# Attention's output phase: seven meetings of all engines a group become three, and two counters hand the work on

## The reference

```python
x = L0_attn_x                                    # 4 groups of 512 tokens, 256 channels
mod = (_silu(L0_c) @ L0_wmod).reshape(L0_c.shape[0], 6, 1, -1)
sa, ca, ga, sb, cb, gb = (mod[:, 0], mod[:, 1], mod[:, 2], mod[:, 3], mod[:, 4], mod[:, 5])
ga = (2 * (ga >= 0) - 1) * jnp.maximum(jnp.abs(ga), 0.25)
h = _layernorm(x, axis=-1) * (1 + ca) + sa
x = x + ga * _L0_attn_ref(h, ...)                # q,k,v with LoRA, RoPE, causal softmax, P.V,
                                                 # then the output projection Wo + LoRA
```

## Time and profile before

| what | value |
|---|---|
| median of 3 runs | 2363.53 us (2359.64 to 2376.82) |
| the profiled execution's own time | 2381.58 us |
| its span | 2379.8 us |
| mean granted TensorE clock | 0.907 |
| busy share of the span: PE, PEld, DVE, ACT, POOL | 83%, 68%, 71%, 61%, 40% |
| chain that ended last, by engine | PE 54%, DVE 18%, ACT 13% |
| attention's output phases, from the span's start | 178.0 to 196.4, 314.3 to 333.6, 451.0 to 469.3, 587.2 to 606.6 us |

### The profile page before, as it was taken

One profiled execution on the slowest core, in us unless ns is written; L12 is line 12 of the kernel. 1 busy time (PEld: TensorE's weight loads), 2 busy tenths in 40 slices (PEclk: granted clock), 3 DMA queues, 4 the chain that ended last, 5 costly groups with the idle time before them and its releaser, 6 DMA issues.

```text
span 2379.8 us, 40957 instructions
## 1 busy us (share of the span) xinstructions
PE 1981.6 (83%) x12115; PEld 1624.2 (68%) x12115; DVE 1693.0 (71%) x3866; ACT 1460.2 (61%) x3963; POOL 954.2 (40%) x1016
## 2 busy tenths in 40 slices
PE   4786868778539847999989999999989998779995
PEld 4565656666427535888877888778877787557772
DVE  5675756666414476999989998899989997744444
ACT  1472736456214345888887888878887887235550
POOL 0120302112053210454544666547655666175551
PEclk8797979879669977999999999999999999889997
DMA  4159472836823412444434444435544452745556
GB/s 128 36 177 355 139 323 89 317 110 237 342 96 107 140 63 79 136 159 149 151 124 142 164 161 139 163 129 170 173 136 149 153 172 80 241 125 154 159 146 263
DMA packets 159654, 385.26 MB, mean 162 GB/s; under 512 B 23184, under 2 KB 84752, under 8 KB 157136
## 3 DMA queue, kind: packets, MB, share of 16 engines
q1 hardware_dynamic: 144944, 342.91, 42.5%
q0 software_dynamic: 14496, 39.73, 4.6%
HBM read 234.86 MB, written 147.71 MB: 161 GB/s over the span
## 4 chain that ended last, share of the span: by engine, by line
PE 54%; DVE 18%; ACT 13%; issue 6%; POOL 2%; DMA 2%; PEldq 1%; DVEq 1%; SPq 1%; ACTq 1%; PEld 1%; POOLq 0%; another core or an unknown queue 0%
PE bank L2077 11%; PE bank L2133 6%; ACT work L692 5%; PE bank L2105 4%; PE bank L2523 4%; DVE cv L2244 3%; PE bank L2126 3%; PE bank L2118 3%; PE bank L1036 2%; PE bank L2560 2%; ACT l_mat L2168 2%; PE bank L2091 2%; DVE nmax L614 2%; PE bank L1065 2%; PE bank L750 1%
## 5 line engine op out<-in xcount | busy, mean ns | idle before, releaser
L2077 PE MATMUL bank<-h_hi,wi 128*128 128x512 f32 x1024 | 404.4, 436 | 1.3 <-ACTq L151 1.3
L2168 ACT ACTIVATE l_mat<-l_mat,cum_tok 128x128 f32<-128x128 f32 x1024 | 315.1, 424 | 0.0
L2244 DVE SCALAR_TENSOR_TENSOR cv<-bank,cw,cv 128x511 f32<-128x511 f32 (+2 forms) x384 | 287.3, 748 | 31.6 <-ACT cv L2174 12.5
L2297 POOL TENSOR_TENSOR xdec<-xdt,dec_tok 128x384 f32<-128x384 f32 x128 | 107.4, 839 | 393.9 <-DVE xdt L2234 360.7
L2312 POOL TENSOR_TENSOR yg<-yd,sgt 128x512 f32<-128x512 f32 x128 | 227.2, 1775 | 46.4 <-DVE yd L2251 46.4
L2133 PE MATMUL bank<-wo,yg 128*128 128x256 f32 x1024 | 242.4, 380 | 1.5 <-POOL yg L2312 1.5
L2077 PEld LDWEIGHTS bank<-h_hi,wi 128*128 128x128 f32 x1024 | 196.0, 191 | 62.6 <-issue 24.1
L2077 PE MATMUL bank<-h_lo,wi 128*128 128x512 f32 x512 | 203.5, 397 | 0.0
L2133 PEld LDWEIGHTS bank<-wo,yg 128*128 128x128 f32 x1024 | 184.8, 191 | 21.9 <-POOL yg L2312 1.9
L2305 POOL TENSOR_TENSOR gates<-gates,sq 128x512 f32<-128x512 f32 x128 | 164.2, 1283 | 70.6 <-ACT sq L2185 70.5
L828 POOL CAST w_hi<-w_raw 128x512 fp32r<-128x512 f32 x32 | 21.1, 659 | 421.9 <-ACTq L151 273.4
(11 more groups left out here) (393 smaller groups left out, 4908.7 us busy)
## 6 DMA issues: line engine op xcount, KB each, us to landing
sorted_rows<-blank SPq DMA_DIRECT2D x16, 4644.0 KB, 33.5
wi<-in_weights_split SPq DMA_DIRECT2D x128, 512.0 KB
l_mat<-running_sums SPq DMA_DIRECT2D x128, 512.0 KB, 4.9
experts_xt<-sorted_rows SPq DMA_DIRECT2D x174, 129.0 KB
experts_got<-chosen_rows SPq DMA_DIRECT2D x32, 512.0 KB, 8.9
wo<-out_weights_normed SPq DMA_DIRECT2D x128, 128.0 KB
w_raw<-in_wi SPq DMA_DIRECT2D x32, 256.0 KB, 2.6
in_weights_split<-w_hi SPq DMA_DIRECT2D x32, 256.0 KB, 2.9
```

What stands on the lines that cost most here:

```text
L2077: mm = e.matmul(dst[:, :], l, r[:, k, tok], start=(n == 0), stop=(n == 3 * KD - 1))
L2168: last = e.activation(part, part, ACT.Relu, bias=cum_tok[:, c, hh, bass.ds(w.g, 1)], scale=-1.0)
L2244: e.scalar_tensor_tensor(out=cv[:, w.two, n:SEQ], in0=PSX[w.two][:, 0:SEQ - n], scalar=cw[:, bass.ds(w.f, 1), TAPS - 1 - n], in1=cv[:, w.t ...
```

## The change

The output phase loses its four inner meetings. Two new semaphores count steps instead: `o_pe`, raised by PE, and `o_dve`, raised by DVE, each a fixed number of times a group (`OUT_PE` = 8, `OUT_DVE` = 6). `heads_high`, which ACT raises, is kept and raised four times a group instead of two.

- DVE normalises tile `i` as soon as PE has folded tile `i`.
- PE transposes two tiles (a half) as soon as DVE has normalised them. A half of 256 tokens goes to banks 4 and 5, the other to banks 6 and 7, each to columns 0 to 255.
- ACT's and DVE's splits work on halves: four instructions of 256 columns each instead of two of 512.
- PE multiplies by the output weights a half at a time, and DVE's tail runs a half at a time.
- There is no meeting after the output projection; one meeting is added at the end of attention, behind the fourth group's tail. A group has three meetings instead of seven.
- The counters `waits_passed_...` of each engine become one counter for all of them; nothing waits on it.

```diff
--- before.py
+++ after.py
@@ -142,7 +142,7 @@
             self.e, self.name, self.meet = e, name, Tally(met)
             self.own = Tally(chain) if chain is not None else None
             self.calls = {stage: Tally(None) for stage in ("norm",)}
-            self.passes, self.waited = sem("waits_passed_" + name), False
+            self.passes, self.waited = sem("waits_passed"), False
 
         def together(self):
 
@@ -473,6 +473,7 @@
     s_s, s_max = sem("scores_done_then_gate_up"), sem("max_done_then_silu")
     s_exp, s_turn, s_pthigh, s_ptev, s_pv = sem("probs_done_then_tanh"), sem("probs_turned_then_hidden_turned"), sem("probs_high"), sem("probs_low"), sem("pv_done_then_down")
     s_otev, s_ohigh = sem("heads_out"), sem("heads_high")
+    o_pe, o_dve = sem("out_steps_pe"), sem("out_steps_dve")
 
 
     QOFF = [0, 128, 384, 768]
@@ -623,20 +624,36 @@
                 probs_low(e, b, HEADS - 1, u)
             v.together()
             v.step(e.reciprocal(rsum[:, :, :], ssum[:, :, :]))
-            v.together()
             for i in range(TT):
                 src = bank[i][:, 0:D].rearrange("p (h s) -> p h s", s=DK)
-                v.own.add(e.tensor_tensor(on[:, i, :].rearrange("p (h s) -> p h s", s=DK), src,
-                                          rsum[:, :, i:i + 1].broadcast_to([P, HEADS, DK]), ALU.mult))
-            v.together()
-            v.together()
-            for k in range(KD):
-                e.wait_ge(s_ohigh, b * KD + k + 1)
-                v.own.add(e.tensor_tensor(hb_lo[:, k, :], bank[4 + k][:, :], hb_hi[:, k, :].bitcast(FP32),
-                                          ALU.subtract))
-            v.together()
-            v.together()
-            tail_dve(v, b, (bank[0], bank[1]), 0, False)
+                e.wait_ge(o_pe, OUT_PE * b + i + 1)
+                e.tensor_tensor(on[:, i, :].rearrange("p (h s) -> p h s", s=DK), src,
+                                rsum[:, :, i:i + 1].broadcast_to([P, HEADS, DK]), ALU.mult).then_inc(o_dve, 1)
+            for half in range(2):
+                for k in range(KD):
+                    e.wait_ge(s_ohigh, 2 * KD * b + KD * half + k + 1)
+                    last = e.tensor_tensor(hb_lo[:, k, half_of(half)], out_bank(half, k),
+                                           hb_hi[:, k, half_of(half)].bitcast(FP32), ALU.subtract)
+                last.then_inc(o_dve, 1)
+            for half in range(2):
+                e.wait_ge(o_pe, OUT_PE * b + TT + 2 + half + 1)
+                for i in (2 * half, 2 * half + 1):
+                    v.own.add(e.tensor_tensor(tail_tmp[:, i, :], token_major((bank[0], bank[1]), i),
+                                              gates[:, 0, b, :], ALU.mult))
+                e.wait_ge(s_dve, v.own.now())
+                for i in (2 * half, 2 * half + 1):
+                    xi = x[:, b * TT + i, :]
+                    v.own.add(e.tensor_tensor(xi, xi, tail_tmp[:, i, :], ALU.add))
+            e.wait_ge(s_dve, v.own.now())
+        v.together()
+
+    OUT_PE, OUT_DVE = TT + 2 + 2, TT + 2
+
+    def half_of(half):
+        return slice(half * SEQ // 2, (half + 1) * SEQ // 2)
+
+    def out_bank(half, k):
+        return bank[4 + KD * half + k][:, 0:SEQ // 2]
 
     def probs_high(e, b, h, u):
         off, size = TOFF[u]
@@ -651,9 +668,7 @@
         e.tensor_tensor(pt_lo[:, h % 2, off:off + size], bank[3 + u][:, 0:size],
                         pt_hi[:, h % 2, off:off + size].bitcast(FP32), ALU.subtract).then_inc(s_ptev, 1)
 
-    ATTN_MEETS = NORM_MEETS + 1 + 2 + 2 + 1 + TAIL_MEETS
-    ATTN_STEPS = (NORM_STEPS + 1 + 1 + TT * (2 + 1 + 3) + 1 + TT + KD
-                  + TAIL_STEPS)
+    ATTN_MEETS = NORM_MEETS + 1 + 1
 
     def attn_act(a):
         e = a.e
@@ -700,13 +715,11 @@
                 probs_high(e, b, HEADS - 1, u)
             attn_out(e, b, HEADS // 4 - 1)
             a.together()
-            a.together()
-            a.together()
-            a.together()
-            for k in range(KD):
-                e.activation(hb_hi[:, k, :], bank[4 + k][:, :], ACT.Copy).then_inc(s_ohigh, 1)
-            a.together()
-            a.together()
+            for half in range(2):
+                e.wait_ge(o_pe, OUT_PE * b + TT + half + 1)
+                for k in range(KD):
+                    e.activation(hb_hi[:, k, half_of(half)], out_bank(half, k), ACT.Copy).then_inc(s_ohigh, 1)
+        a.together()
 
     def attn_out(e, b, g):
         e.wait_ge(s_pv, b * HEADS + 4 * g + 4)
@@ -794,23 +807,27 @@
             t.together()
             for i in range(TT):
                 for g in range(4):
-                    e.matmul(bank[i][:, g * 4 * DK:(g + 1) * 4 * DK], ot[:, g, i * P:(i + 1) * P], fold[:, :],
-                             start=True, stop=True)
-            t.together()
-            t.together()
-            for k in range(KD):
-                for i in range(TT):
-                    e.transpose(bank[4 + k][:, i * P:(i + 1) * P], on[:, i, k * P:(k + 1) * P], ident[:, :])
-            for _ in range(2):
-                t.together()
-            for i in range(TT):
-                n = 0
-                for k in range(KD):
-                    for l, r in ((hb_hi, we_hi), (hb_lo, we_hi), (hb_hi, we_lo)):
-                        e.matmul(token_major((bank[0], bank[1]), i), l[:, k, i * P:(i + 1) * P], r[:, k, QKV:4 * D],
-                                 start=(n == 0), stop=(n == 3 * KD - 1))
-                        n += 1
-            t.together()
+                    mm = e.matmul(bank[i][:, g * 4 * DK:(g + 1) * 4 * DK], ot[:, g, i * P:(i + 1) * P], fold[:, :],
+                                  start=True, stop=True)
+                mm.then_inc(o_pe, 1)
+            for half in range(2):
+                for i in (2 * half, 2 * half + 1):
+                    e.wait_ge(o_dve, OUT_DVE * b + i + 1)
+                    for k in range(KD):
+                        mm = e.transpose(out_bank(half, k)[:, i % 2 * P:(i % 2 + 1) * P], on[:, i, k * P:(k + 1) * P],
+                                         ident[:, :])
+                mm.then_inc(o_pe, 1)
+            for half in range(2):
+                e.wait_ge(o_dve, OUT_DVE * b + TT + half + 1)
+                for i in (2 * half, 2 * half + 1):
+                    n = 0
+                    for k in range(KD):
+                        for l, r in ((hb_hi, we_hi), (hb_lo, we_hi), (hb_hi, we_lo)):
+                            mm = e.matmul(token_major((bank[0], bank[1]), i), l[:, k, i * P:(i + 1) * P],
+                                          r[:, k, QKV:4 * D], start=(n == 0), stop=(n == 3 * KD - 1))
+                            n += 1
+                mm.then_inc(o_pe, 1)
+        t.together()
 
     def attn_pool(g):
         e = g.e
@@ -830,9 +847,8 @@
...
-            for _ in range(ATTN_MEETS - NORM_MEETS - TAIL_MEETS - 1):
-                g.together()
             g.together()
+        g.together()
...
-    stages = {"attn": ((attn_sync, attn_act, attn_pool, attn_dve, attn_pe), 4 * GROUPS * ATTN_MEETS),
+    stages = {"attn": ((attn_sync, attn_act, attn_pool, attn_dve, attn_pe), 4 * (GROUPS * ATTN_MEETS + 1)),
```

## The result

| | before | changed |
|---|---|---|
| median | 2364.87 us | 2324.29 us (2321.65 to 2333.0) |
| ratio, 95% interval | | 0.9836 (0.981 to 0.9863) |
| the profiled execution: its span, mean granted clock | 2379.8 us, 0.907 | 2319.8 us, 0.925 |

The changed kernel is 1.6% faster, by 41 us between the medians. I had forecast 20, and a range for 8 in 10 that ended at 2329 us.

What follows compares the result with a forecast made beforehand. The prediction took each output phase as one serial chain; 3.4 us (hand-over) and 1.55 us (tail) over four groups, less 0.15, gave about 20 us off the 2363.5 us median: 2343.5 us, 8-in-10 range 2329 to 2355.

Steps and rivals of the forecast that it cites:

- What bounds the phase, and that all of it comes off the end: Output phase: one serial chain, 18.33 us in the first group, 19.39 in the second; time taken out comes off the end.
- DMAs and scatter: Experts after attention: DMA work moves up by 15 us, GpSimd's scatter by 20, leaving 4 of 9 us of room.
- The overlap: Output phase: engines run beside each other, saving 3.4 us in the hand-over and 1.55 in the tail per group.
- The hand-over: Fold's end to projection: transposes 1.1, split 1.25, crossings 0.15, so 2.5 us against 5.9, 3.4 us less a group.
- the crossings: Hand-over: two passages between engines, at 0.02 to 0.1 us, taken as 0.15 us for both together.
- The tail's halves: DVE's tail: half runs under the projection's second half, 1.43 + 0.05 us stay, 1.55 us less a group.
- The 0.8 us that I worked out from it: Semaphore increments on completed matmuls: 26 ns each, eight a group, estimated 0.8 us over four groups, making the saving 19 us.
- Nothing gained and nothing lost at an unchanged clock: Projection: the same 24 matmuls in two halves without a stop between, 5.49 us in the first group, 5.28 in the second.
- The sum: Whole kernel: 4 x (3.4 + 1.55) - 0.15 = 19.65, say 20 us saved, with the clock as before.
- a rival: PE's clock in the output phase comes back earlier or stays up: 3 to 14 us more, 2329.5 to 2340.5 us; chance 0.28.
- The rivals on the other side: Gain partly lost, 2351.8 or 2354.9 us, chance 0.17; dearer crossings, 2391.5 us, 0.03; end set elsewhere, 2363.5 us, 0.02.
- The adapter product: Next group's product on PE behind the projection: 3.71 us, still hidden; in a rival, at 1.2 GHz, DVE waits 1.1 us.

Runs made afterwards that it cites:

- wide_warm_before: The kernel before, all meetings kept, with dead matmuls in PE's two gaps of each phase and a fold of 128 columns at a time; 2349.74 us, 0.992.
- wide_fold: The changed kernel with a fold of 128 columns at a time, the 64 wanted ones written twice; 2326.01 us, 0.9836.
- no_halves: The changed kernel with its two semaphores but no halves: transposes, split, projection and tail each done whole; 2348.76 us, 0.994.
- tail_whole: The changed kernel with only the tail's halves undone: DVE's tail starts when all four tiles are projected; 2336.67 us, 0.9889.
- fine_tail: The changed kernel with projection and tail handed over a tile at a time, each tile in its own bank; 2330.1 us, 0.986.
- warm_before: The kernel before, all meetings kept, with five and seven dead matmuls in PE's two gaps of each output phase; 2355.85 us, 0.9965.

## Why the prediction was right and wrong

**What bounds the phase, and that all of it comes off the end: right.** 31.0 us went in the phases, and attention as a whole lost that and more. DMAs and scatter followed: in the first pair the first scatter came 31.9 us earlier from the span's start and 32.8 from the first norm, where attention was 33.0 us shorter, and the first experts took 316.6 and 316.9 us.

**The overlap: right.** At a clock of 1.00 in both, four phases of the old order take 60.8 us (`wide_warm_before`) and of the new one 41.5 (`wide_fold`). That is 19.3 us where I had 19.65: 4.9 in each of three groups, where I had 4.95, and 4.6 in the fourth, where the added meeting takes 0.3 us and not 0.15 (10.6 against 10.3). The terms moved a little against each other:
- The hand-over is 2.11 us at 0.50 and 1.71 at 1.00, for 2.5 priced. Four transposes took 0.87 or 0.46 for 1.1, ACT's copy 0.39 for 0.40, DVE's two 0.77 for 0.83, the crossings 0.08 for 0.15.
- The tail's halves brought 1.3 us, for 1.55.
- A crossing from PE by a semaphore is in the chain as "issue" of 0.02 us, and so is one from ACT. The Trainium skill ("TensorE: Matmul & The Clock Gate", The cost: per-tile semaphore tail) has 26 ns for each increment; nothing here contradicts that, but since the crossing from ACT shows the same 0.02 us, no row shows the increment by itself. The 0.8 us that I worked out from it would be too small to see in the sum.

**"Nothing gained and nothing lost at an unchanged clock": the step that failed.** The condition didn't hold. The sum put the clock at nothing. But the projection with the rest of the tail takes 5.63 us in a group where the clock fell and 4.75 where it stayed, where I had 5.4 and 1.5, 6.9 in all. The phases of before lose 15.3 us to the clock (76.1 less 60.8), those of the changed kernel 3.6 (45.1 less 41.5). The difference, 11.7 us, was not in my sum. I had it as a rival: 3 to 14 us, chance 0.28. Its mechanism was right and the 11.7 us lie in its range; what was wrong was to leave it out of the sum and its chance. The time that it gave, 2329.5 to 2340.5 us, was not low enough for the first measurement (2324.3) and holds for the second (2331.3).

Some of the 11.7 may be luck. Within the fold the clock fell in 11 of the 16 phases of the old order and in 3 of the 8 of the changed one, though the fold's instructions are the same; in the other 5 of the old order it fell in the gap behind the fold. A fall costs a phase of the changed kernel 2.5 us (12.77 against 10.24). If its folds had it as often as the old ones, it would lose an estimated 6.9 us and not 3.6, and the gain would be 3 us less. In `no_halves`, `tail_whole` and `fine_tail`, with the same fold, the clock fell within it in 8 of 12 phases. What closed gaps took away is the other kind of fall: where the fold itself ended at 1.00, the clock fell behind it in 5 of 5 phases before and in none of 5 after.

I put it low for two reasons. The first was the fold of the second group, where the clock fell with PE busy; I concluded that closed gaps need not help. That reading was correct, `warm_before` and `wide_fold` bear it out, but it speaks of part of the phases only. Of the eight phases of the changed kernel that were profiled, three had a fall; of the sixteen of the old order, all had. The second was the Trainium skill's rule (same page, Part 4: PE-mode transpose) that transposes don't engage the full clock. Here the clock was at 1.00 under transposes that followed a fold at 1.00 (312.91 to 314.62), and stayed so into the projection. The trace of before had spoken against my use of the rule already: the earlier trace rows has ten transposes at 2.4 GHz, and the 0.50 under the second group's transposes was there from the fold on. The rule may hold for what raises the clock; that some transposes between two dense pieces pull it down is not what these rows show.

The same page of the Trainium skill (Part 1: The HAM clock gate) has the throttle follow how busy PE was, and idle gaps bring it back. What it says of gaps does not cover the fold, where the profile shows no idle time of PE (5.00 of 5.00 us) and a granted clock of 0.73.

**The other 3.7 us**, between the phases, I had not foreseen at all. The three parts, 19.3 + 11.7 + 3.7, are attention's 34.7 us; they add up by the way they were taken.

**The rivals on the other side** have nothing for them. The chain has no crossing above 0.04 us in the phase. The adapter product was hidden, and no wait for it appears behind a tail.

## What to carry to other kernels

Where TensorE's granted clock differs between repeats of one piece of code, price a change at both levels, and give the higher level a chance by how many of the stalls the change takes away. Here the clock added 11.7 us to an overlap worth 19. Before adding dead matmuls to keep the clock up, see in a profile whether the fall is removed or only comes later: for the fold a wider moving operand removed it at 0.05 us a fold, though the total was not shown to be shorter for it, and fillers between the phases mostly moved it.

## What the runs showed of the hardware

- TensorE's clock fell from 2.4 to 1.2 GHz inside a run of 32 records of fp32 matmuls with 64 columns, without idle time in the profile (5.00 of 5.00 us busy, 0.73 granted). With 128 columns and the same weight loads it stayed at 2.4 GHz in 24 of 24 phases, and the run took 3.81 us instead of 3.76.
- Sixteen 128x128 fp32 transposes in a row took 1.94 us at a granted clock of 1.00 and 3.58 at 0.52 (third group, changed and before).
- A hand-over by drain and meeting against one by a plain semaphore: at the fold's end 0.16 us (181.87 to 182.03) against 0.02. The rest of what `no_halves` gained in the phases came from work that the meetings had kept apart and, in its fourth group, from the clock (15.3 us at 0.89 against 16.9 at 0.70).
